# Order of the attention maxima at the end of the first feed-forward stage of a macaron block

## What is computed

```
x = x + 0.5 * ffn(layernorm(x), W_up, W_gate, W_down)
x = x + attention(layernorm(x), Wq, bq, Wk, bk, Wv, bv)
x = x + 0.5 * ffn(layernorm(x), W_up, W_gate, W_down)

ffn(x):        hidden = silu(x @ up.T) * (x @ gate.T);  return hidden @ down.T
               (1024 hidden features; up, gate, down are ternary: round(W / mean|W|) cut to -1..1, times mean|W|)
attention(x):  16 heads of 16 features, 4 groups of keys and values, so 4 heads share one;
               scores = q k^T / 4, causal mask, softmax over the keys, times v
```

## Time and profile before

| | |
|---|---|
| median of three runs | 591.67 us |
| the profiled execution | 591.82 us, of which 590.1 us is its span (first to last instruction) |
| TensorE matmuls busy | 558.4 us, 95% |
| VectorE busy | 479.8 us, 81% |
| ScalarE busy | 400.3 us, 68% |
| GpSimd busy | 170.2 us, 29% |
| chain that ended last | TensorE 73%, VectorE 18% |
| mean granted TensorE clock | 0.997 |

### The profile page before, as it was taken

The page is one execution under the profiler, slowest core; times in us unless marked ns, Lnnn a source line. Parts: engine busy times, 40 slices in busy tenths (PEclk is TensorE's granted clock), DMA queues, the critical chain, the costliest instruction groups (busy, mean ns, idle before and its releaser), DMA issues.

```text
span 590.1 us, 12391 instructions
## 1 busy us (share of the span) xinstructions
PE 558.4 (95%) x4244; PEld 344.3 (58%) x4244; DVE 479.8 (81%) x1861; ACT 400.3 (68%) x717; POOL 170.2 (29%) x264
## 2 busy tenths in 40 slices
PE   2889999999999989999999999997999999999998
PEld 2346565555666755666666656554455565566566
DVE  6898978989875889898989897995797688756654
ACT  5857665674655368798888888886666665674642
POOL 3115201101530035454546463665401101100100
PEclk9999999999999999999999999998999999999999
DMA  8711101100105151423323323212201212111112
GB/s 313 223 26 37 21 19 34 36 19 19 37 18 126 40 112 57 94 81 69 95 57 102 84 66 84 68 49 38 37 1 36 72 40 69 37 55 54 36 37 72
DMA packets 72222, 37.90 MB, mean 64 GB/s; under 512 B 35520, under 2 KB 71616, under 8 KB 72128
## 3 DMA queue, kind: packets, MB, share of 16 engines
q1 hardware_dynamic: 72160, 37.11, 24.3%
HBM read 18.22 MB, written 10.49 MB: 49 GB/s over the span
## 4 chain that ended last, share of the span: by engine, by line
PE 73%; DVE 18%; ACT 3%; issue 2%; POOL 2%; DMA 2%; SPq 1%; DVEq 0%; POOLq 0%; ACTq 0%
PE bank L1167 33%; PE bank L1179 17%; DVE sm_out L984 7%; PE bank L1266 5%; PE bank L1323 4%; PE bank L1334 4%; PE bank L1293 4%; PE bank L1339 2%; PE bank L1348 2%; PE bank L1143 1%; DVE hid L853 1%; DVE stats L733 1%; POOL xn L413 1%; DVE hl L868 1%; DVE q_hl L972 1%
## 5 line engine op out<-in xcount | busy, mean ns | idle before, releaser
L984 DVE CUSTOM_DVE_ANT_0 sm_out<-bank,mask 128x256 f16<-128x256 f32 (+1 forms) x512 | 151.3, 352 | 16.9 <-PE bank L1293 16.1
L486 ACT ACTIVATE silu<-bank,w_scale 128x512 f32<-128x512 f32 x128 | 87.5, 684 | 112.9 <-PE bank L1167 112.9
L853 DVE SCALAR_TENSOR_TENSOR hid<-silu,h_unit,bank 128x512 f32<-128x512 f32 x128 | 95.0, 743 | 63.8 <-ACT silu L486 63.5
L1179 PE MATMUL bank<-wT_down,hh 128*128 128x256 f16 x512 | 118.3, 273 | 2.5 <-DVE hl L868 2.3
L1179 PE MATMUL bank<-wT_down,hl 128*128 128x256 f16 x512 | 118.2, 273 | 0.0
L1167 PE MATMUL bank<-xh,wT_up 128*128 128x512 f16 x256 | 98.0, 383 | 1.0 <-DVE xl L797 0.7
L868 DVE TENSOR_TENSOR hl<-hid,hh 128x512 f16<-128x512 f32 x128 | 98.6, 770 | 0.0
L1167 PE MATMUL bank<-xh,wT_gate 128*128 128x512 f16 x256 | 97.0, 379 | 1.6 <-DVE hid L853 1.6
L1167 PE MATMUL bank<-xl,wT_up 128*128 128x512 f16 x256 | 98.0, 383 | 0.0
L1167 PE MATMUL bank<-xl,wT_gate 128*128 128x512 f16 x256 | 97.0, 379 | 0.0
L422 POOL TENSOR_TENSOR xnl<-xn,xnh 128x1024 f16<-128x1024 f32 x13 | 28.3, 2179 | 213.2 <-ACT xn L525 177.8
(11 more groups left out here) (134 smaller groups left out, 791.7 us busy)
## 6 DMA issues: line engine op xcount, KB each, us to landing
q_st<-q_scratch SPq DMA_DIRECT2D x32, 256.0 KB
q_scratch<-q_hl SPq DMA_DIRECT2D x16, 256.0 KB, 2.2
out_dram<-x SPq DMA_DIRECT2D x7, 512.0 KB, 3.0
x<-in_x_dram SPq DMA_DIRECT2D x1, 3072.0 KB, 15.5
k_scratch<-k_hl SPq DMA_DIRECT2D x16, 128.0 KB, 2.4
k_st<-k_scratch SPq DMA_DIRECT2D x16, 128.0 KB
x<-in_x_dram SPq DMA_DIRECT2D x2, 512.0 KB, 4.4
shared<-in_w_up_t_dram SPq DMA_DIRECT2D x2, 512.0 KB, 6.7
```

The lines of the kernel that those rows point to most:

```text
L486: act.activation(silu[:, e % 2, :], U[e % 2][:, :], ACT.Silu, scale=w_scale[:, 0:1]).then_inc(silu_ready, 1)
L853: dve.scalar_tensor_tensor(out=hid[:, e % 4, :], in0=silu[:, e % 2, :], scalar=h_unit[:, 0:1], in1=GT[e % 2][:, :], op0=ALU.mult, op1=ALU. ...
L984: ins = dve.tensor_tensor_reduce(sm_out[:, i, cols], SM[i][:, cols], mask[:, S - size:S], -1.0 / MAX_UNIT, -MASKED, ALU.add, ALU.min, rowm ...
L1179: ins = pe.matmul(ACC[t % 2][:, 0:D], part[:, par, e, t * P:(t + 1) * P], wT_down[:, e, :], start=(e == 0 and part is hh), stop=(e == NE - ...
```

## The change

TensorE: the maxima products of group 0 go ahead of the last chunk's first down products, those of group 1 behind their first two halves; groups 2 and 3 follow the projections of t = 0 and t = 1, and group 4 (with the wait for the second sequence's load) follows the projection of t = 2, ahead of the last tile's down products. Before the first of them stand a wait for the load and one for the last hidden tile. VectorE: the maxima of groups 0 and 1 go ahead of the loop over the tiles; in the loop the maxima of group t + 2 come last, behind the residual and the low part. Both `attention()` functions begin one group later. No other stream is edited.

```diff
--- before.py
+++ after.py
@@ -908,18 +908,19 @@
                 chunk(NC - 2, 0, True, None if ph else next_norm)
                 chunk(NC - 1, 1, True, None if ph else attention_start)
                 hidden_low(64 * ph + 63, 1, NE - 1)
+                if ph == 0:
+                    first_row_max(0)
+                    first_row_max(1)
                 for t in range(TT):
 
-                    if ph == 0 and t < 3:
-                        first_row_max(t)
                     residual(NC - 1, t)
                     if ph == 0:
-                        if t == 2:
-                            first_row_max(3)
                         if t == 0:
                             key_low(1)
                         elif t < 3:
                             query_low(1, t - 1)
+                        if t < 3:
+                            first_row_max(t + 2)
 
             def projection_ends(e):
 
@@ -1092,8 +1093,7 @@
                     row_max(n, n // G, n % G, i)
 
             def attention():
-                for n in (4, 5):
-                    first_row_max(n)
+                first_row_max(5)
                 row_max(6, 1, 2, 0)
 
 
@@ -1231,26 +1231,30 @@
                 chunk(NC - 2, 0, True, None if ph else next_norm)
                 chunk(NC - 1, 1, True, None if ph else attention_start)
 
+                if ph == 0:
+                    pe.wait_ge(st_loaded[0][0], 16 * N_ST)
+                    pe.wait_ge(hid_ready, 64)
+                    max_scores(0, 0, 0)
                 pe.wait_ge(hl_ready, 64 * (ph + 1) - 4)
                 down_half(NC - 1, 1, 0, 0)
                 down_half(NC - 1, 1, 1, 0)
+                if ph == 0:
+                    max_scores(1, 0, 1)
                 pe.wait_ge(hl_ready, 64 * (ph + 1))
                 for t in range(TT):
-                    if ph == 0:
-
-                        if t == 0:
-                            pe.wait_ge(st_loaded[0][0], 16 * N_ST)
-                        if t < 3:
-                            max_scores(t, 0, t)
                     if t > 1:
                         down_half(NC - 1, 1, t, 0)
                     down_half(NC - 1, 1, t, 1)
                     if ph == 0:
                         if t == 2:
                             max_transposes(0, 0)
-                            max_scores(3, 0, 3)
                         if t < 3:
                             project_all(1, t)
+                        if t < 2:
+                            max_scores(t + 2, 0, t + 2)
+                        if t == 2:
+                            pe.wait_ge(st_loaded[0][1], 16 * N_ST)
+                            max_scores(4, 1, 0)
 
             def project(c, m, part):
 
@@ -1426,8 +1430,6 @@
                             output_transposes(b, k, 1, (onorm_ready, 2 * b + 1) if last else (val_ready, c + 3))
 
             def attention():
-                pe.wait_ge(st_loaded[0][1], 16 * N_ST)
-                max_scores(4, 1, 0)
                 pe.wait_ge(res_done, NT + 2)
                 max_transposes(0, 1)
                 val_transposes(1, (qkv_lo, 5))
```

## The result

Nine runs of each kernel, taken in turn: the changed kernel 592.91 us in the median (592.17 to 593.56), the kernel before 591.05 (590.30 to 592.29). The ratio is 1.0028, 95% interval 1.0018 to 1.0037: slower by 0.28%, some 1.7 us. A second comparison gave 1.0023 (1.0011 to 1.0034); there and in experiments 5 and 6, which share its runs of the kernel before, four executions at 605 to 3230 us (three of the kernel before, one of experiment 6) are left out as slow.

A forecast was written before the change was run, and what follows sets the result against it. TensorE and VectorE were taken to hand the path to and fro, neither bounding it alone. The late transpose gave +1.34 us, all else 0: 593.0 us against a median of 591.67, range 591.7 to 594.4.

The forecast's parts named there:

- Step 1: Group 0's products go ahead of the first down products; its maxima start 1.51 us earlier, a gain paid back later.
- Steps 2 to 4: Last chunk: TensorE stalls 0.3 us on group 1's third bank; VectorE's gap before the keys is 1.25 us, 0.94 before.
- step 7: Waits for loads: group 0's products need the q_st copy, costing 0 to +0.4 us; taken as nothing.
- Step 5: VectorE: group 4's maxima stand ahead of the last residual, which starts at 207.43 us instead of 206.09.
- Step 6: TensorE waits for the last residual before the maxima transpose, a new 1.9 us stall; all behind moves by 1.34 us.
- The walk's 1.34: Sum of the walk through the new order: +1.34 us from the late maxima transpose, 0 at all other places.
- B: Same delay, and TensorE's clock falls in some runs after the new stall, 0.9 us more: 593.9; chance 0.25.
- C: First attention pair: the delay is taken up later, 0.3 us or less is left: 591.9; chance 0.15.
- D: VectorE's early start survives up to group 5's maxima, a gain of 1.17 us: 590.5; chance 0.10.

The follow-up runs named there:

- experiment 5: The filled kernel: changed kernel plus nine unused matmuls in TensorE's wait for the last residual; 1.0022 to the kernel before; the changed kernel again, unfilled, 1.0023.
- experiment 6: Changed kernel with the second maxima transpose in bank 3 ahead of the last down products, and group 5's products among the scores; 0.9982 to the kernel before.
- experiment 3: Kernel before with only group 0's maxima products moved ahead of the last chunk's first down products, VectorE's order unchanged; 1.0007 to the kernel before.
- experiment 1: Changed kernel with, on VectorE only, the last residual back ahead of group 4's maxima; 1.0004 to the kernel before.
- experiment 4: Changed kernel with group 4's products and maxima back at their old place in both streams; 0.9989 to the kernel before.
- experiment 2: Changed kernel with, on TensorE only, group 5's maxima products ahead of the wait for the last residual; 1.0017 to the kernel before.

## Why the prediction was right

The forecast was 593.0 us, against 592.91 measured, and +1.34 us, against 1.66 (0.28% of 591.05; interval 1.1 to 2.2). That the absolute time fits to 0.1 us is luck: the kernel before came out at 591.05 and not at the 591.67 that I started from, and the step was a few tenths larger than mine, so two misses cancel. The direction and the mechanism were right, point by point:

- **Step 1**, that the early start is paid back: shown alone by experiment 3.
- **Steps 2 to 4**, the new gaps and stalls: each was found at its place. The gap before the keys is 1.13 us where I had 1.25, and the first stall, TensorE's on group 1's third bank, lies inside the merged row of those products, 0.90 us long where the others are 0.82: 0.08 where I had 0.3, since these products themselves came 0.25 late (step 7).
- **Step 5**, the last residual behind group 4: the step that decides, as forecast. Swapping the two on VectorE (experiment 1) takes the loss away to within what can be told, and leaving group 4 where it was (experiment 4) too.
- **Step 6**, TensorE's stall of 1.9 us: it is 1.77 in the record and carries all behind it along. Experiment 6 takes it out and gains.
- **Step 7**, the load: I took nothing, "the middle". It was late:

```profile
186.03 3.80 DMA q_st<-q_st
```

The row is of the chain of the changed kernel: the copy on `q_st` landed 3.80 us after its issue began, near the longest landing of the earlier trace rows (4.2). Group 0's products start at 189.88 although the x transposes in front of them leave TensorE free at some 189.64 (188.77 and the 0.87 from 188.89 to 189.76 in the earlier trace rows). VectorE had 0.24 us to spare and lost nothing, and TensorE's later wait for group 1's bank took up the rest; where that wait is missing, in experiment 3, the 0.24 is still there at 240 us. Taking the middle of the landings was the wrong choice, without an effect on this sum.
- **The size.** The walk's 1.34 is what the filled kernel's profile shows, in which the clock stays up (experiment 5: +1.32). The rest, 0.2 to 0.3 us in the profiles, is the fall of the clock, the term that I left out of the sum. The times don't resolve it: without a fall the step is 1.13 us in the filled kernel and 1.66 in the changed one.

**The rivals.** B came in by half: the clock fell behind the stall, in both profiled executions of the changed kernel. But I priced it at 0.9 us, between 0.4 and 1.95, and it is worth 0.3 at most, for VectorE was the engine that set the pace from group 5 on: from its start on group 5 to the next x transposes it is 3.17 us in the kernel before, in the filled one and in both profiles of the changed one, whatever the clock. C is out: by the clocks of the two profiles, not counted from the mark, the x transposes are 1.49 us late (213.66 against 212.17), and of this nothing is taken up later; the rows at 402 us still show +1.65 (404.30 against 402.65, the latter from the profile of the kernel before). D is out in the changed kernel, as res3 came 1.8 us later than it would have needed. Experiment 6 reaches by another way what D asks for, group 5's products ready when VectorE comes free, and the gain that D put at 1.17 is there: 1.1 in the times.

**Why the two profiled executions differ by so little**, 0.35 us. These are single executions, each with one fall of the clock, at different places. At the start of the last sequence's second outputs the changed kernel is 1.65 us behind; from there, in the changed kernel,

```profile
404.30 0.64 PE L1338 MATMUL bank<-hh,val 128*32 128x256 f32 x8
...
412.30 0.66 PE L1352 MATMUL bank<-ident,shared 128*128 128x128 f32 x4 [0.33 <-DVE shared L1076]
```

8.00 us go by to the output transposes. In the kernel before the same two are 9.27 us apart, since there the clock fell after 407 us; its TensorE timeline:

```profile
402.65 0.64 PE L1334 MATMUL bank<-hh,val 128*32 128x256 f32 x8
...
411.92 0.66 PE L1348 MATMUL bank<-ident,shared 128*128 128x128 f32 x4 [0.34 <-DVE shared L1075]
```

So a single execution hides 1.27 of the 1.65 us.

## What to carry to other kernels

When work is moved up in one engine's stream, look at what it now stands in front of, and who waits for that: here 2.2 us of reductions, not urgent, went ahead of a 0.4 us residual on which another engine's whole queue hung. Filling an idle gap of an engine was worth nothing here while the product that it needed next ended when it did (experiment 3). If a wait comes from a shared buffer and not from the data, try another buffer beside another order: here both were faster than the kernel before, and which is better can't be told.

## What the runs showed of the hardware

TensorE's clock fell from 2.4 to 1.2 GHz after a stretch with a stall of 1.77 us and one of 0.56 (changed kernel, at 209.8 and 210.2 us), and in the kernel before at 407 us without any gap over 1 us (its waits there were 0.81 and 0.63). The Trainium skill's page "TensorE: Matmul & The Clock Gate", section "HAM oscillation — how this bites in real kernels", names longer gaps than these; here the measurement decides.

The fall is not in every execution of one kernel. Of 33 runs of the kernel before, 22 had a mean granted clock of 1.000 and a median of 590.71 us, 11 had 0.997 and 591.72. In the second comparison it was 13 with 590.65 and 12 with 592.16. That is 1.0 to 1.5 us for one fall; where it lay is known for profiled executions alone: at 407 to 409 us in the kernel before and in experiments 2, 4 and 6, and in the kernel before it cost 1.27. At 210 us, where VectorE sets the pace, a fall cost 0.3 at most. A fall that comes more often under one kernel than under another thus moves a ratio by as much as the effects told of here. Why the three runs of the changed kernel without a fall (592.10 to 592.48 us) are not below those with a mean of 0.997 (six, median 592.19) was not found out.
